# Two 12-bit float32r parts instead of three bfloat16 parts for q and k, in two halves of the array's rows

## The reference, cut to what matters

```python
x = x + 0.5 * ffn(layernorm(x));  x = x + attn(layernorm(x));  x = x + 0.5 * ffn(layernorm(x))
# attn:
q, k, v = heads(x @ Wq.T), heads(x @ Wk.T), heads(x @ Wv.T)   # 64 (batch, head) pairs, 1024 x 8 each
q, k = rope(q), rope(k)
score = einsum('bqd,bkd->bqk', q, k)                          # causal, / sqrt(8)
out = softmax(score) @ v;  return out @ Wo.T
```

## Time and profile before

| | us |
|---|---|
| median of 3 runs | 913.25 (910.16 to 917.05) |
| span of the profiled execution, first to last instruction | 855.6 |
| the median less this span | 57.65 |
| busy in the span: PE, DVE, ACT, POOL | 779.7, 610.9, 507.4, 315.4 |
| mean granted TensorE clock, share of full | 0.945 |

### The profile page before, as it was taken

The page is one execution under the profiler, slowest core; times in us unless marked ns, Lnnn a source line. Parts: engine busy times, 40 slices in busy tenths (PEclk is TensorE's granted clock), DMA queues, the critical chain, the costliest instruction groups (busy, mean ns, idle before and its releaser), DMA issues. The chain is left out here.

```text
span 855.6 us, 17846 instructions
## 1 busy us (share of the span) xinstructions
PE 779.7 (91%) x5570; PEld 427.9 (50%) x5570; DVE 610.9 (71%) x1919; ACT 507.4 (59%) x1229; POOL 315.4 (37%) x603
## 2 busy tenths in 40 slices
PE   9889999887899999999999999999999997689995
PEld 8888896543233333333333333333333335579884
DVE  4657774698668777788878878788787722856663
ACT  2166651673247767667667766766777684146662
POOL 6177742475104223223322422331242231056753
PEclk8699999998569999999999999999999998789998
DMA  8721113065332033033113303312320001122110
GB/s 271 270 57 50 54 33 117 23 169 159 57 57 45 14 57 57 10 49 58 34 26 57 53 6 57 58 22 36 57 41 18 3 1 34 73 70 50 52 42 26
DMA packets 27989, 51.84 MB, mean 61 GB/s; under 512 B 7552, under 2 KB 19200, under 8 KB 26496
## 3 DMA queue, kind: packets, MB, share of 16 engines
q1 hardware_dynamic: 21296, 41.04, 20.7%
q0 software_dynamic: 4096, 8.69, 3.8%
q10 hardware_dynamic: 2512, 1.06, 0.5%
HBM read 35.40 MB, written 14.97 MB: 59 GB/s over the span
## 5 line engine op out<-in xcount | busy, mean ns | idle before, releaser
L1448 DVE CUSTOM_DVE_ANT_0 cst<-psS,mask_row 128x768 bf16<-128x768 f32 (+7 forms) x512 | 364.7, 756 | 100.2 <-PE psS L1308 97.6
L1412 ACT ACTIVATE prob<-psST 128x512 f32<-128x512 f32 (+3 forms) x750 | 317.3, 495 | 158.9 <-PE psST L1339 155.2
L1353 PE MATMUL a_psO<-prob,vs 128*32 128x512 f32 (+3 forms) x1536 | 166.7, 506 | 2.8 <-ACT prob L1412 1.7
L1532 POOL TENSOR_TENSOR a_gate<-a_zeros 1x1 f32<-1x1 f32 x128 | 23.7, 185 | 333.7 <-ACT prob L1412 333.7
L1339 PE MATMUL psST<-a_qs,ks 75*128 75x512 bf16 (+1 forms) x480 | 123.7, 327 | 5.9 <-ACT prob L1412 3.5
L1308 PE MATMUL psS<-ks,a_qs 72*128 72x512 bf16 (+2 forms) x480 | 119.0, 337 | 5.6 <-DVE a_rowmax L1448 5.5
L777 POOL DMA_INDIRECT tok<-rows,f_there_number x64 | 61.8, 966 | 86.0 <-DVE f_number L489 42.0
L1308 PEld LDWEIGHTS psS<-ks,a_qs 72*128 72x128 bf16 x480 | 35.6, 99 | 101.1 <-DVE a_rowmax L1448 33.0
L1308 PE MATMUL psS<-ks,qs 72*128 72x512 bf16 (+3 forms) x288 | 75.8, 354 | 6.7 <-DVE a_rowmax L1448 6.5
L1533 POOL TENSOR_SCALAR_AFFINE_SELECT prob<-prob 128x512 f32<-128x512 f32 x128 | 80.3, 627 | 0.0
L1339 PE MATMUL psST<-qs,ks 75*128 75x512 bf16 (+3 forms) x270 | 73.4, 346 | 2.7 <-ACT prob L1412 1.7
(11 more groups left out here) (183 smaller groups left out, 1066.1 us busy)
## 6 DMA issues: line engine op xcount, KB each, us to landing
a_qs<-q_split SPq DMA_DIRECT2D x60, 96.0 KB
rows<-tok SPq DMA_DIRECT2D x8, 536.0 KB, 4.9
ks<-k_split SPq DMA_DIRECT2D x32, 128.0 KB
qs<-q_split SPq DMA_DIRECT2D x36, 96.0 KB
q_split<-p_part SPq DMA_DIRECT2D x24, 128.0 KB, 2.4
k_split<-p_part SPq DMA_DIRECT2D x24, 128.0 KB, 2.4
ks<-k_split SPq DMA_DIRECT2D x16, 192.0 KB
tok<-x_after_first SPq DMA_DIRECT2D x4, 536.0 KB, 5.4
```

Of the source, the lines that this page charges most:

```text
L1353: last = nc.tensor.matmul(psO[32 * h:32 * h + 32, c0:c0 + w], vs[r][:, j, h, :], prob[:, u % RING, h, 0:w], start=(j == 0), stop=(u + 1 in ...
L1412: nc.scalar.activation(prob[:, u % RING, h, 0:w], score_buffer(s, u * QH + h)[:, 0:w], ACT.Exp, scale=SCALE).then_inc(exp_done, 1)
L1448: last = nc.vector.tensor_tensor_reduce(out=out[:, a * CH:a * CH + width], in0=ps[:, a * CH:a * CH + width], in1=mask_row[:, S - width:], ...
```

## The change

q and k are split in KINDS = 2 parts: ACT's copy writes the high one rounded to float32r (12 bits), one subtraction gives the low one. All parts are stored as 4-byte floats. A head's stack has 2 x 2 x 8 = 32 rows, then a row of zeros, then two rows for the maximum, and heads 0, 1 lie in partitions 0 to 63, heads 2, 3 in 64 to 127 (the two *lanes*). Every tile and score product reads 33 or 35 rows of one lane as float32r, which addresses half of the array's rows.

```diff
-KINDS = 3
+KINDS = 2
+LANE = 64
+LANES = 2
+LH = QH // LANES
 PR = KINDS * KINDS * DK
-MR = KINDS
+MAX_AT = PR + 1
+ROWS_PLAIN = PR + 1
+ROWS_MAX = PR + 1 + KINDS
...
-        n.ks = [sb(f"ks{i}", [PR + MR, QH * S], BF16) for i in range(RING)]
+        n.ks = [sb(f"ks{i}", [P, LH * S]) for i in range(RING)]
...
-STACK_DMAS = 2 * KINDS - 1 + KINDS * NCH
+STACK_DMAS = LANES * (3 + KINDS * NCH)
...
+    part = [[n.prob[:, 2, KINDS * k:KINDS * (k + 1), :] for k in range(2)],
+            [sb(f"part{k}", [P, KINDS, CH]) for k in range(2)]]
...
         def subtract_hi(g, k):
-            for i in range(2):
-                dve.wait_ge(hi_done[i], g + 1)
-                wait(dve, lo_done[i], g - 1)
-                nc.vector.tensor_tensor(rest[i][k], rot[i][k], part[i][k][:, 0, :],
-                                        ALU.subtract).then_inc(rest_done[i], 1)
-        def subtract_mid(g, k):
-            dve.wait_ge(mid_done[0], g + 1)
-            nc.vector.tensor_tensor(part[0][k][:, 2, :], rest[0][k], part[0][k][:, 1, :],
+            dve.wait_ge(hi_done[0], g + 1)
+            nc.vector.tensor_tensor(part[0][k][:, 1, :], rot[0][k], part[0][k][:, 0, :],
                                     ALU.subtract).then_inc(lo_done[0], 1)
...
-                nc.scalar.activation(part[i][k][:, 0, :], rot[i][k], ACT.Copy).then_inc(hi_done[i], 1)
+                nc.scalar.activation(part[i][k][:, 0, :].bitcast(F32R), rot[i][k], ACT.Copy).then_inc(hi_done[i], 1)
...
-    tiles = [((h, h + 1), i) for i in range(CB) for h in range(0, QH, 2)]
+    tiles = [((h, h + LH), i) for i in range(CB) for h in range(LH)]
+    LANE_TURNS = [lane * LH + k for k in range(LH) for lane in range(LANES)]
-    tiles += [((h,), i) for i in (CB, TB - 1, CB + 1, TB - 2) for h in range(QH)]
+    tiles += [((h,), i) for i in (CB, TB - 1, CB + 1, TB - 2) for h in LANE_TURNS]
...
+    def q_part(r, h, rows, q, w):
+        top = h // LH * LANE
+        return qs[r][top:top + rows, q_col(h, q):q_col(h, q) + w].bitcast(F32R)
...
+    def in_lanes(jobs):
+        found, lane, left = [], 0, {}
+        def put_score(u):
+            nonlocal lane
+            heads = left.setdefault(u, list(LANE_TURNS))
+            h = ([k for k in heads if k // LH != lane] or heads)[0]
+            heads.remove(h)
+            lane = h // LH
+            found.append(("score", u, (QH - 1 - len(heads), h)))
...
+            elif what == "tile":
+                work = products(arg)
+                work.sort(key=lambda k: (k[1] // LH == lane, k[0]))
+                for at, product in enumerate(work):
+                    found.append(("tile", arg, (product, at == 0, at == len(work) - 1)))
+                    lane = product[1] // LH
...
-            sp.dma_start(max_rows(r, half), maxT[half][:, :]).then_inc(max_loaded[half], 16)
+            for lane in range(LANES):
+                for m in range(KINDS):
+                    sp.dma_start(max_row(r, half, lane, m),
+                                 maxT[half][lane * LH * CB:(lane + 1) * LH * CB, m, :]).then_inc(max_loaded[half], 16)
...
-            pe.wait_ge(split_done, 2 * s + half + 1)
-            nc.tensor.transpose(ps[:, 0:P // 2].bitcast(BF16), maxparts[:, :], n.identb[:, :]).then_inc(use_done, 1)
+            pe.wait_ge(use_read, ready)
+            nc.tensor.matmul(ps[0:MP, 0:P], rowmax[:, half, :],
+                             n.c("ident"), start=True, stop=True).then_inc(use_done, 1)
...
-            nc.vector.tensor_copy(maxT[half][:, :],
-                                  ps[0:MP, 0:P // 2].bitcast(BF16)).then_inc(use_read, 1)
+            nc.vector.tensor_scalar(maxT[half][:, 0, :].bitcast(F32R), ps[0:MP, 0:P], -1.0, None,
+                                    ALU.mult).then_inc(max_split, 1)
+            dve.wait_ge(max_split, 2 * s + half + 1)
+            nc.vector.scalar_tensor_tensor(maxT[half][:, 1, :], ps[0:MP, 0:P], -1.0, maxT[half][:, 0, :],
+                                           ALU.mult, ALU.subtract).then_inc(use_read, 1)
```

More of the change, by code:

```diff
@@ L8 @@
 F32 = mybir.dt.float32
+F32R = mybir.dt.float32r
 BF16 = mybir.dt.bfloat16
@@ L802, in ffn @@
         return rows_written
-STACK_DMAS = 2 * KINDS - 1 + KINDS * NCH
+STACK_DMAS = LANES * (3 + KINDS * NCH)
 PART_ROWS = KINDS * DK
 def stack_parts(n, s, q, k):
[L812 to L817, removed]
+    for lane in range(LANES):
+        heads = ds(s * QH + lane * LH, LH)
+        top = lane * LANE
+        for there, first, last in ((0, 0, 2), (2, 1, 2), (3, 0, 1)):
+            here = top + there * DK
+            yield (k[here:here + (last - first) * DK, :],
+                   n.k_dram[first * DK:last * DK, heads, :].rearrange("d h t -> d (h t)"))
         for ch in range(NCH):
-            yield (q[c * PART_ROWS:(c + 1) * PART_ROWS, ch * QH * CH:(ch + 1) * QH * CH],
-                   n.q_dram[:, ch, ds(s * QH, QH), :].rearrange("d h t -> d (h t)"))
+            for c in range(KINDS):
+                here = top + c * PART_ROWS
+                yield (q[here:here + PART_ROWS, ch * LH * CH:(ch + 1) * LH * CH],
+                       n.q_dram[:, ch, heads, :].rearrange("d h t -> d (h t)"))
 def load_stacks(sp, n, s, q, k, loaded):
@@ L1206, in q_col, with k_part, products, heads_in_turn @@
     def q_col(h, q):
-        return (q // CH * QH + h) * CH + q % CH
+        return (q // CH * LH + h % LH) * CH + q % CH
+    def q_part(r, h, rows, q, w):
+        top = h // LH * LANE
+        return qs[r][top:top + rows, q_col(h, q):q_col(h, q) + w].bitcast(F32R)
+    def k_part(r, h, rows, key, w):
+        top = h // LH * LANE
+        return ks[r][top:top + rows, h % LH * S + key:h % LH * S + key + w].bitcast(F32R)
+    def products(t):
+        heads, i = tiles[t]
+        return [(a * CH + c0, h, i, c0, min(CH, (i + 1) * P - c0))
+                for a, h in enumerate(heads) for c0 in range(0, (i + 1) * P, CH)]
+    def in_lanes(jobs):
[7 more added lines that the diff above has]
+            found.append(("score", u, (QH - 1 - len(heads), h)))
+        jobs = list(jobs)
+        while jobs:
+            what, arg, arg2 = jobs.pop(0)
+            if what == "score":
+                put_score(arg)
+            elif what == "tile":
[4 more added lines that the diff above has]
+                    lane = product[1] // LH
+            else:
+                found.append((what, arg, arg2))
+        return found
+    def heads_in_turn(jobs):
+        return {(u, k[0]): k[1] for what, u, k in jobs if what == "score"}
     def sb(name, shape, dt=F32):
@@ L1324, in turn_out, with score @@
             last.then_inc(use_done, 1)
-        def score(s, r, u, h):
+        def score(s, r, u, place):
             ch, j, q0, w = units[u]
-            if u in half_start and h == 0:
+            k, h = place
+            if u in half_start and k == 0:
                 half = half_start.index(u)
-                pe.wait_ge(max_loaded[half], (s + 1) * 16)
-            m = u * QH + h
+                pe.wait_ge(max_loaded[half], (s + 1) * 16 * LANES * KINDS)
+            m = u * QH + k
             if s < NST - 1 or m < 3:
@@ L1360, in stage @@
             k = 0
-            for what, arg, arg2 in plan(first, last):
+            for what, arg, arg2 in stage_jobs[first, last]:
                 if what == "score":
@@ L1386, in _ @@
         k = 0
-        for what, arg, arg2 in opening():
+        for what, arg, arg2 in opening_jobs:
             if what == "score":
@@ L1425, in stage @@
                     copy_out(s, 0)
-                exps(s, u)
+                exps(s, u, head_at[first, last])
         for i in range(2):
@@ L1540, in stage @@
                     if not last:
-                        split(s + 1, 0, base(s, first) + half_ready["first" if first else "middle", 0],
-                              2 * s + 2)
                         values(s + 1, (r + 1) % RING)
                 mask(s, u)
-            if not last:
-                split(s + 1, 1, base(s, first) + half_ready["first" if first else "middle", 1], 2 * s + 3)
         pool.wait_ge(cleared, 1)
```

172 lines of the change are left out of this document (75 added, 97 removed).

## The result

The changed kernel takes **1171.37 us** (median of 4 runs, 1159.93 to 1186.07), the kernel before 914.95 (4 runs): a ratio of **1.269**, 95% interval 1.262 to 1.276. The ratio is of the executions that ran at the higher clock, two of the four (1159.93 and 1163.39, middle 1161.66). I had forecast 903 and a range of 878 to 985.

The account below looks back on a forecast made before the run. PE was taken as the fullest engine, in a ring of waits with DVE and ACT. Stages -1.5, opening -4 and `project` -4.5 made -10 on the 855.6 us span; plus 57.65, 903 us, range 878 to 985.

Parts of the forecast that it names:

- The stages run at full clock: Attention stages: read from the old profile, full clock with PE busy 95%, DVE 80%, ACT 70%; 30.2 us per stage.
- the clock stays at 1.2 GHz in the stages: Rival for the stages: weighs +8 us and lanes +4 to +8 per stage, run over 1,080 us; chance 0.05.
- A stage at full clock: Each of fourteen attention stages: sum of the stage terms -0.1 us, -1.5 us for all fourteen.
- Columns and the overlap: Tile and score products: float32r takes 0.22 us per 512 columns; row halves overlap, eight products in five steps per wide unit.
- Weights: Weight loads in stages: float32r load 0.11 us; bare after a weigh, costing 0.06 us in each of 12 units.
- no overlap: Rival and stage end: halves run one after the other, +1.0 us per stage, +14 in all, 923 us; chance 0.18.
- changes around `turn_out`: Two `turn_out` per stage: array goes to full rows and back, four changes at +0.05 us, +0.2 per stage.
- four DMAs for one of a maximum: Loads of maxima: some 2 us more, put at nothing since scores were 9 us away.
- DVE or the exponential's latency then stops PE elsewhere: Stages: 0.65 us saved per wide unit falls into time its reductions (2.3 us) and exponentials (2.06 us) still need.
- The opening: Lower-clock opening, 218 to 249 us: PE-bound, five steps for eight give 8 us, half kept: -4; ends 0 and -8.
- `project`: Groups in `project`: DVE loses two subtractions, PE bounds at 5.2 us instead of 5.97, -4.5; ends 0 and -5.
- The median lies 57.65 above the span, and I carry that.: Whole run: 57.65 us outside the profiled span of 855.6 us, added unchanged to the forecast span of 845.6 us.

Follow-up runs that it names:

- 64-row stage: Changed kernel with every float32r tile and score product reading all 64 rows of its half, not 33 and 35: 975.98 us, ratio 1.069.
- bfloat16 kernel with 64 rows: Changed kernel with bfloat16 parts instead of float32r and all 64 rows of each half read: 915.83 us, ratio 1.003.
- The kernel before with few rows: Kernel before with tile products cut from 72 rows to 33 and score products from 75 to 35: 1214.88 us, ratio 1.335.
- bfloat16 halves: Changed kernel with bfloat16 parts and 64 rows in each half: 915.83 us with two parts of a maximum, 895.17 with one.
- two kernels over 128 rows, without halves: Changed kernel's float32r products over all 128 rows: 953.98 us; bfloat16 parts, all heads in one 128-row range, one part of a maximum: 909.46 us.

## Why the prediction was wrong, step by step

**The failed step: "The stages run at full clock", carried over to the changed kernel.** I had the case as a rival, "the clock stays at 1.2 GHz in the stages", and gave it 0.05. My ground against it was that the last stage keeps 0.98 without tiles. But that stage's scores still have 75 rows and its weighs 128: it tests fewer products, not thinner ones. The ground for it, fewer columns streaming, was the wrong one too. PE was busier than before, and the old kernel with all its columns but 33 rows lost the clock as well. What the change takes away is rows per product. The rival's price, +8 for weighs and +4 to +8 for the halves, was too low: +19.4 (49.6 - 30.2). Fourteen such stages would be 272 us; the clock came back now and then, and the attention lost 251.6. PE's 28.4 us of work in the 64-row stage are 48.3 in the changed kernel's, and DVE and ACT wait for all of it.

The Trainium skill advises to keep TensorE busy to have the full clock ("TensorE: Matmul & The Clock Gate", Why this matters for your kernels). Here a stage with PE busy 97% ran at 0.50 and one with 81% (the bfloat16 kernel with 64 rows) at 1.00; the measurement decides. The same section says of a single matmul over 32 rows that it takes the time of one over 128; column for column the traces agree at an equal clock (512 columns take 0.43 us at 0.50 with 33 rows in "The kernel before with few rows" and with 72 in the opening of the kernel before), but the clock was not equal.

**A stage at full clock, -0.1 us predicted.** +2.9 measured with two parts of the maxima. Columns and the overlap: right; 512-column products over one range of rows start from 0.23 us apart. *Weights*: mis-sized. I charged 0.06 us at 12 loads; float32r cost 2.4 us a stage with overlap and, without it, 4.4 us of PE's busy time. Behind a weigh alone, the second product of a half starts 0.33 us after the first in the 64-row float32r kernel (310.40, 310.73) and 0.22 in the bfloat16 one (425.33, 425.56). Even the end "no overlap", +1.0, was far short of +3.5 to +4.0 (33.8 to 34.3 less 30.3). The +0.2 for changes around `turn_out` had no row behind it, and no run takes it apart from the rest. *Maxima*: "four DMAs for one of a maximum" stood at nothing, with scores "9 us away"; a score waited up to 1.0 us for the last of them. With the second instruction of `copy_max`, put at +0.3, they are 0.6 to 0.9 a stage. "DVE or the exponential's latency then stops PE elsewhere": right. In the bfloat16 halves PE has 25.1 us of work instead of 28.9, and the stage is 29.96 or 30.85 us instead of 30.32.

**The opening, -4 predicted.** From the first reduction to the third turn of the maxima the kernel before takes 48.8 us, the changed one 50.9, the 64-row kernel 49.3: nothing gained, and the changed kernel lies beyond the end at 0. The two bfloat16 kernels with 64 rows in both halves take 46.0 and 45.1, near what I had forecast, but the two kernels over 128 rows, without halves, take 44.7 (float32r) and 41.7 (bfloat16). The clock goes with this: in the opening it is at 0.50 for 17.1 and 13.7 us in these two, for 34.2 in the kernel before and for 47 in the changed one. What the halves alone give there, no run separates.

**`project`, -4.5 predicted.** -6.4 measured, groups 4.8 us apart (201.47 to 206.27) and bound by PE, as said; 5.2 was too high, and the gain lies beyond the end at -5. POOL's memsets before it, which I put at nothing, seem to hold up DVE: one instruction of 8 elements takes 1.57 us (171.50 us) where its like take 0.17, and ends with the last of them.

**"The median lies 57.65 above the span, and I carry that."** Wrong: a span lies 1.7 us below its time; the profiled execution was another, faster one than those timed. The forecast took no harm, since all differences are of stretches that both executions have. But what I called time outside the span were feed-forward blocks that ran slower in every other execution of which a span is on record.

## What to carry to other kernels

- Before cutting the rows of a matmul that fills most of the time, ask what the clock does. Rows of zeros against ones add no columns and no instructions: here 64 rows instead of 33 gave back 186 us.
- With few columns per load, price the load at every product, and price a type by its load as well as by its columns.
- A shift inside a softmax needs no second part; look for such terms before splitting them exactly.

## What the runs showed of the hardware

- The granted clock went with the rows that products read, at the same columns and instructions. In bfloat16 it was from 300 to 700 us 0.52 with 33 and 35 rows, 0.57 with these in two halves, 0.99 to 1.00 with 64 in both halves, and 1.00 with 72 and 75 and with 128. In float32r it was 0.53 with 33 and 35 in two halves, 0.67 with 33 and 64, 0.94 to 0.98 with 64 in both halves, 0.79 with 64 in one half, 1.00 with 128. Rows of zeros counted. What in them counts, and where the border lies, I did not try. The values between 0.50 and 1.00 are means of stretches at the two levels, and the same stages ran both ways within one execution (41.0 and 49.6 us, 34.3 and 57.5).
- float32r: one instruction per product, 512 columns in 0.43 us at 1.2 GHz, which is one column per cycle, and a load of 128 columns in 184 ns (bfloat16 97) at full clock. Products in the upper and the lower 64 rows start 0 to 0.01 us apart.
- While POOL cleared rows with memsets of 3.5 us each, DVE instructions of 8 elements took up to 3.53 us instead of 0.17.
